# A fourth score tile turned through DRAM, its low part on VectorE, a new hand-written order and no loops, in an attention and gated-FFN kernel

## The reference, cut to what matters

```python
q = proj(Wq, bq) * scale; k = proj(Wk, bk); v = proj(Wv, bv)
q = apply_rotary(pos, q); k = apply_rotary(pos, k)
sim = jnp.einsum('bhid,bhjd->bhij', q, k)
sim = jnp.where(causal, -jnp.finfo(sim.dtype).max, sim)
attn = jax.nn.softmax(sim, axis=-1)
out = jnp.einsum('bhij,bhjd->bhid', attn, v)
out = out.transpose(0, 2, 1, 3).reshape(b, n, INNER)
x = x + ga * (out @ Wo + bo)
```

## Time and profile before

| | us |
|---|---|
| median of 3 runs | 970.95 |
| the profiled execution | 968.9 |
| its span | 967.0 |
| PE busy | 934.2 (97%) |
| DVE busy | 735.9 (76%) |
| ACT busy | 673.4 (70%) |
| POOL busy | 774.9 (80%) |

### The profile page before, as it was taken

The page is one execution under the profiler, slowest core; times in us unless marked ns, Lnnn a source line. Parts: engine busy times, 40 slices in busy tenths (PEclk is TensorE's granted clock), DMA queues, the critical chain, the costliest instruction groups (busy, mean ns, idle before and its releaser), DMA issues.

```text
span 967.0 us, 20178 instructions
## 1 busy us (share of the span) xinstructions
PE 934.2 (97%) x5667; PEld 833.6 (86%) x5667; DVE 735.9 (76%) x1582; ACT 673.4 (70%) x1354; POOL 774.9 (80%) x555
## 2 busy tenths in 40 slices
PE   6989999999999999999999999999999999878898
PEld 5878998888889989989998888889989989767787
DVE  6766877778878877787877877887878777867544
ACT  5766766677677767676767677777777676757763
POOL 2468988898898988898889888998889888795653
...
GB/s 256 163 137 137 179 166 142 159 182 154 140 136 175 167 136 158 179 167 150 145 156 174 169 150 133 183 148 139 156 170 168 158 147 171 177 95 44 1 44 46
DMA packets 108978, 141.63 MB, mean 146 GB/s; under 512 B 12948, under 2 KB 80084, under 8 KB 108884
## 3 DMA queue, kind: packets, MB, share of 16 engines
...
...
## 4 chain that ended last, share of the span: by engine, by line
PE 87%; DVE 3%; POOL 3%; issue 2%; ACT 2%; DMA 1%; SPq 0%; POOLq 0%; DVEq 0%; ACTq 0%
PE ps_r L1565 18%; PE ps_r L1564 18%; PE ps_r L1563 18%; PE ps_s L1563 7%; PE ps_s L1565 7%; PE ps_s L1564 7%; PE ps_t L1728 5%; PE ps_s L1570 1%; PE ps_s L1573 1%; PE ps_r L1570 1%; PE ps_r L1572 1%; PE ps_r L1668 1%; ACT probs L1046 1%; POOL pT_lo L782 1%; DMA wmod_a<-in_L_wmod 1%
## 5 line engine op out<-in xcount | busy, mean ns | idle before, releaser
L1046 ACT ACTIVATE probs<-ps_s,neg_max 128x128 f32<-128x128 f32 (+7 forms) x256 | 189.8, 742 | 84.5 <-DVE neg_max L1451 82.3
L764 POOL TENSOR_TENSOR swapped<-swapped,sin_sb 128x512 f32<-128x512 f32 x124 | 161.2, 1300 | 94.4 <-DMA swapped<-straight 94.1
L1451 DVE CUSTOM_DVE_ANT_0 ps_s<-ps_s,mask_wide 128x128 f32<-128x128 f32 (+7 forms) x256 | 193.6, 756 | 14.8 <-PE ps_s L1565 12.4
L782 POOL TENSOR_TENSOR pT_lo<-side_p,pT_hi 128x1024 fp32r<-128x1024 f32 (+2 forms) x93 | 195.3, 2131 | 0.7 <-ACT pT_hi L1035 0.7
L773 POOL TENSOR_TENSOR qk_lo<-swapped,qk_hi 128x512 fp32r<-128x512 f32 x124 | 159.4, 1297 | 19.7 <-ACT qk_hi L930 19.6
L767 POOL TENSOR_TENSOR swapped<-swapped,qk_cos 128x512 f32<-128x512 f32 x124 | 161.3, 1301 | 10.5
L1563 PE MATMUL ps_s<-qk_hi 128*128 128x512 f32 (+4 forms) x384 | 142.1, 370 | 2.4 <-ACT probs L1046 2.3
L1379 DVE STREAM_TRANSPOSE squares<-probs 128x1024 f32<-128x1024 f32 (+2 forms) x93 | 103.1, 1109 | 51.6 <-ACT probs L1046 48.4
L1565 PE MATMUL ps_r<-pT_hi,v_lo 128*128 128x512 f32 (+3 forms) x384 | 133.0, 346 | 0.0
L1564 PE MATMUL ps_r<-pT_lo,v_hi 128*128 128x512 f32 (+3 forms) x384 | 132.6, 345 | 0.0
L1565 PE MATMUL ps_s<-qk_hi,qk_lo 128*128 128x512 f32 (+4 forms) x384 | 131.4, 342 | 0.0
...
## 6 DMA issues: line engine op xcount, KB each, us to landing
...
```

The costliest lines, as they stand in the source:

```text
L764: pool.tensor_tensor(swapped[:, q, :], swapped[:, q, :], sin_sb[:, at_], ALU.mult).then_inc(rotated, 1)
L782: pool.tensor_tensor(turned_at(t, 0, t + 1)(pT_lo).rearrange("p k (i c) -> p k i c", c=SQUARE), from_squares(side_p[t], t)[:, t::-1, :, :] ...
L1046: nc.scalar.activation(halved(t, probs[:, P_AT[step] * P:(P_AT[step] + t + 1) * P]), score_rows(step, t), ACT.Exp, bias=neg_max[:, t:t + 1 ...
L1451: nc.vector.tensor_tensor_reduce(rows, rows, halved(t, mask_wide[:, SEQ - n_keys:SEQ]), -1.0, -MASKED, ALU.add, ALU.min, accum_out=neg_max ...
```

## The change

Tile 4 is turned aside as well, in units 0 to 30: its five transposes on TensorE, their two copies on ScalarE and two subtractions on VectorE are gone. In their place stand a transposition of squares on VectorE (`side:7-`), a write and four reads on SyncE (`side:7-`, `back:7-`), one copy of 640 keys per row on ScalarE (`side:7-`), and one subtraction of 640 on VectorE (`lower:7-`), for which the function `side_lower` was there and not used. All plans of the loop and of units 29 to 31 are written anew. ScalarE issues the loads of the weights. The loops are gone: units 1 to 31 stand one behind another, with constants as wait values.

```diff
-SIDE = (7, 6, 5)
+SIDE = (7, 6, 5, 4)
...
-TENSOR_PLAN = """scores:0 turn:6.0- make:K0+ make:Q0+ turn:7.0- scores:1 make:P0- scores:2 turn:7.1- make:K1+ make:Q1+
-        turn:0.0 scores:3 make:W00- scores:4 make:P1- turn:2.0 scores:5 make:W01- make:W10- turn:4.0 scores:6
-        make:W11- scores:7 make:V0 make:V1"""
...
+TENSOR_PLAN = """make:K0+ turn:6.0- scores:0 make:Q0+ scores:1 make:P0- scores:2 make:K1+ make:Q1+ turn:0.0 scores:3
+        make:W00- turn:2.0 scores:4 make:P1- make:W01- scores:5 make:W10- make:W11- scores:6 turn:4.0 make:V0
+        scores:7 make:V1"""
+SCALAR_PLAN = """exp:7- out:K0+ turn:6.0- out:Q0+ exp:0 side:5- high:P0- exp:1 out:K1+ exp:2 out:Q1+ side:7- high:K0+
+        turn:0.0 split:V turn:2.0 exp:3 high:Q0+ split:Q exp:4 split:K high:P1- side:1 | exp:5 raw:K split:O
+        high:K1+ exp:6 raw:Q high:V0 turn:4.0 side:3 raw:V high:Q1+ high:V1 raw:O"""
+VECTOR_PLAN = """side:7- max:0 cos:K0+ turn:6.0- cos:Q0+ max:1 | low:P0- max:2 side:1 cos:K1+ cos:Q1+ lower:7- max:3
+        sum:W00- turn:0.0 max:4 side:3 split:Q turn:2.0 low:P1- sum:W01- max:5 sum:W10- max:6 side:5 sum:W11-
+        low:V0 max:7 turn:4.0 low:V1"""
+POOL_PLAN = """side:5- rotate:K0+ rotate:Q0+ low:K0+ split:V low:Q0+ rotate:K1+ rotate:Q1+ split:K low:K1+ split:O |
...
-SYNC_PLAN = """swap:K0+ swap:Q0+ | side:1 back:1 side:3 swap:K1+ swap:Q1+ back:3 side:5 back:5 raw:K raw:Q raw:V raw:O"""
+SYNC_PLAN = """side:7- swap:K0+ swap:Q0+ back:7- | side:1 back:1 swap:K1+ side:3 swap:Q1+ back:3 side:5 back:5"""
...
+            def load_raw(ps, j, n):
+
+                if j == WO:
+                    act.wait_ge(w_ready[WV], ps.passes(n + 1))
+                    src = wo_t[:, bass.ds(ps.passes(n) * 2, 2), :]
+                else:
+                    act.wait_ge(w_ready[WO if j == WV else j], ps.passes(n))
+                    src = w_t[j][:, :, bass.ds(ps.passes(n) * 2 * DH, 2 * DH)]
+                act.dma_start(w_buffers[j][0], src).then_inc(raw_ready[j], 16)
...
             run(Span(0, 1))
-            with act.Fori(0, LAST) as i:
-                run(Span(1, 1 + UNITS, i))
-            run(Span(1 + LAST * UNITS, ALL_UNITS + 1))
+            run(Span(1, ALL_UNITS + 1))
```

More of the change, by code:

```diff
@@ L130 @@
 PLANS_29 = {
-    SYNC_PLAN: """swap:K0+ swap:Q0+ | side:1 back:1 side:3 swap:K1+ swap:Q1+ back:3 load:0 side:5 back:5 load:1"""}
+    SYNC_PLAN: """side:7- swap:K0+ swap:Q0+ back:7- | side:1 back:1 swap:K1+ side:3 swap:Q1+ back:3 load:0 side:5 back:5
+        load:1"""}
 PLANS_30 = {
-    TENSOR_PLAN: """scores:0 turn:6.0- make:K0+ make:Q0+ turn:7.0- scores:1 make:P0- scores:2 turn:7.1- make:K1+ make:Q1+
-        turn:0.0 scores:3 make:W00- scores:4 make:P1- turn:2.0 scores:5 make:W01- make:L0 make:W10- make:L1
-        turn:4.0 scores:6 make:L2 make:W11- make:L3 scores:7 make:L4 make:L5""",
@@ L138 @@
[L138 to L142, removed]
+    TENSOR_PLAN: """make:K0+ turn:6.0- scores:0 make:Q0+ scores:1 make:P0- scores:2 make:K1+ make:Q1+ turn:0.0 scores:3
+        make:W00- turn:2.0 scores:4 make:P1- make:W01- scores:5 make:W10- make:L0 make:W11- make:L1 scores:6
+        turn:4.0 make:L2 make:L3 scores:7 make:L4 make:L5""",
@@ new lines @@
+    SCALAR_PLAN: """exp:7- out:K0+ turn:6.0- out:Q0+ exp:0 side:5- high:P0- exp:1 out:K1+ exp:2 out:Q1+ side:7- high:K0+
+        turn:0.0 turn:2.0 exp:3 high:Q0+ float:0 exp:4 float:1 high:P1- side:1 float:2 exp:5 out:L0 high:K1+
+        out:L1 exp:6 turn:4.0 out:L2 side:3 out:L3 high:Q1+ out:L4 out:L5""",
+    VECTOR_PLAN: """side:7- max:0 cos:K0+ turn:6.0- cos:Q0+ max:1 low:P0- max:2 side:1 cos:K1+ cos:Q1+ lower:7- max:3
+        sum:W00- turn:0.0 max:4 side:3 turn:2.0 largest:0 low:P1- sum:W01- max:5 sum:W10- max:6 side:5 sum:W11-
@@ L151 @@
-    SCALAR_PLAN: """out:K0+ exp:7- turn:6.0- exp:0 out:Q0+ side:5- turn:7.0- turn:7.1- float:3 high:P0- turn:0.0 exp:1 exp:2
-        high:P1- exp:3 turn:1.0 turn:1.1 turn:2.0 exp:4 gated:0 out:D0 turn:3.0 exp:5 turn:3.1 turn:4.0 out:D1
[L153 to L156, removed]
@@ L157 @@
-    SYNC_PLAN: """load:4 load:5"""}
+    TENSOR_PLAN: """make:K0+ make:Q0+ scores:0 turn:6.0- scores:1 make:P0- scores:2 turn:0.0 scores:3 make:W00- make:P1-
+        turn:1.0 scores:4 turn:1.1 turn:2.0 make:W01- make:X scores:5 make:D0 turn:3.0 make:W10- turn:3.1
+        turn:4.0 make:W11- scores:6 make:D1 turn:5.0 scores:7 make:D2 turn:5.1""",
+    SCALAR_PLAN: """out:K0+ exp:7- turn:6.0- exp:0 out:Q0+ side:5- float:3 high:P0- exp:1 turn:0.0 exp:2 side:7- exp:3
+        high:P1- turn:1.0 turn:1.1 turn:2.0 exp:4 gated:0 out:D0 turn:3.0 exp:5 turn:3.1 turn:4.0 out:D1 exp:6
+        turn:5.0 out:D2 turn:5.1""",
@@ L160 @@
+    VECTOR_PLAN: """side:7- max:0 turn:6.0- max:1 low:P0- max:2 largest:2 turn:0.0 max:3 lower:7- sum:W00- largest:3 low:P1-
+        turn:1.0 turn:1.1 max:4 moments:0 turn:2.0 sum:W01- width:X max:5 turn:3.0 sum:W10- turn:3.1 turn:4.0
+        sum:W11- max:6 max:7 turn:5.0 turn:5.1""",
+    SYNC_PLAN: """side:7- back:7- load:4 load:5"""}
 ENDING = {
```

38 lines of the change are left out of this document (8 added, 30 removed).

## The result

The changed kernel takes 978.95 us (median of 6 runs, 978.31 to 985.3), the kernel before 970.65 beside it: 8.3 us slower, where 13 us faster was forecast. The ratio over all runs is 1.0104, with a 95% interval of 1.0084 to 1.0124; that of the medians alone is 1.0086. The two longest runs (985.3 and 984.82) had a mean granted clock of 0.983 and 0.985, the other four 0.994 or 0.995.

A forecast was written before the change was run, and what follows sets the result against it. TensorE's own work was taken as the bound: 968.9 us, less 16.0 for transposes, plus 2.9 for late V0, gave 955.8; with 2.05 from profiled run to median, 957.9, rounded 958. The range was 951 to 980.

The forecast's parts named there:

- What bounds the kernel: Middle units: TensorE's own work sets the 25.90 us per unit, so what leaves TensorE is gained until a wait appears.
- the transposes: TensorE, units 2 to 30: five transposes gone, 0.55 us per unit, 29 units, 16.0 us gained.
- The low part of tile 4: VectorE before P1: waits about 0.1 us for GpSimd, within 0.3 us of slack, so no stall.
- both sums: From V0's end: GpSimd ends Q0's first operation 14.1 us later, VectorE's low part comes due 14.07 later; trusted to 0.3.
- rival B: Some units stall as GpSimd's phase shifts with weight splits and DMAs; 965, or 963 to 969 us; chance 0.2.
- rival C: GpSimd begins Q0's second operation before VectorE's low part; P1 1.0 us late every unit, 987 us; chance 0.2.
- D: Rival: tile 4's read-backs come late through SyncE's order or fuller DMA queues, delaying ScalarE; 968 to 975 us; chance 0.08.
- The sums: V0 waits for VectorE's sum of W10: 0.1 us late in 29 units, +2.9 us, ends 0 and 4.4.
- The ends: Unit 1 and behind unit 30, where TensorE already has gaps: nothing gained, 2 us to either side.
- ScalarE's and SyncE's DMAs: ScalarE's four weight loads a pass: 0 taken, 3 us kept for the range; SyncE's added transfers and later swap: nothing.
- The loops: Removing the seven rounds of the loops gives TensorE nothing; VectorE's and ScalarE's register arithmetic goes, which helps the margins.

The follow-up runs named there:

- q0_small: The changed kernel with GpSimd's two operations on Q0 cut to 16 of 512 elements from unit 2 on, leaving out most of that rotation; 964.86 us.
- combo_sums: Changed kernel with previous orders in units 1, 30, 31, tile 4's low part one place earlier, SyncE's weight loads, VectorE's W10 and W11 sums earlier; 1000.56 us.
- flat_actload: The kernel before, without loops and with ScalarE issuing the weight loads; tile 4 and the order as before; 972.66 us.
- order_only: The changed kernel (its order, no loops, ScalarE's weight loads) with tile 4 turned on TensorE again; 984.82 us.

## Why the prediction was wrong

**What bounds the kernel, and the transposes: right.** A unit without a stall is 25.56 in the changed kernel and 25.58 in q0_small. With the 0.17 of V0 and V1 off that is 25.4, the forecast's 25.35 within 0.06.

**The low part of tile 4: this step failed**, where it said "I take no stall here". The duration and the exclusion held. So did both sums, for one unit: V0 ended at 352.98, GpSimd's first operation of Q0 at 367.12, 14.14 later (forecast 14.1), and VectorE began L1389 at 367.06, 14.08 later (14.07). VectorE's sum held on: 14.0 to 14.2 in all middle units but one. GpSimd's did not: 14.1 to 15.8. What failed is that the sum starts GpSimd on ScalarE's high Q1, as if GpSimd then stood waiting, and lets it run on from there without a wait. POOL 14 us earlier, in the unit without a stall and in the one with it:

```profile
355.64 1.30 POOL L767 TENSOR_TENSOR qk_lo<-swapped,qk_hi 128x512 fp32r<-128x512 f32 x1 [1.04 <-ACT qk_hi L922]
```

```profile
379.68 1.31 POOL L767 TENSOR_TENSOR qk_lo<-swapped,qk_hi 128x512 fp32r<-128x512 f32 x1
380.94 1.30 POOL L750 TENSOR_TENSOR wo_lo<-wo_raw,wo_hi 128x512 fp32r<-128x512 f32 x1
382.19 1.29 POOL L767 TENSOR_TENSOR qk_lo<-swapped,qk_hi 128x512 fp32r<-128x512 f32 x1
```

V0 ended at 352.98 and at 378.47. In the first GpSimd waits and takes low Q1 2.66 later; in the second it comes from the split of Wo and takes it 3.72 later, 1.06 late, and everything up to Q0 with it. The split is not the whole of it. Shortly before, GpSimd had waited 2.33 us for the swapped keys of K1 (to 374.30), where 1.3 to 1.6 is usual, and that left it no pause to take up the split in. The five units of the middle with both, a split of Wo and a wait of some 2.1 us or more, stall 3.6 us together; the two with such a wait and no split (L1389 at 678.94 and 782.30) don't stall.

In four other units low Q1 began on time, and GpSimd waited for a DMA afterwards, 0.44 to 1.66 us: twice for the swapped keys of K0, twice for tile 5, whose read-back ScalarE's copy awaits. ACT and POOL in the worst, whose P1 came 1.1 late at 525.06:

```profile
517.53 0.85 ACT L1027 ACTIVATE pT_hi<-side_p 128x768 fp32r<-128x768 f32 x1 [1.80 <-DMA side_p<-side_out]
```

```profile
518.45 1.84 POOL L776 TENSOR_TENSOR pT_lo<-side_p,pT_hi 128x768 fp32r<-128x768 f32 x1 [1.66 <-ACT pT_hi L1027]
```

All four come 15 to 19 us behind ScalarE's loads, and have 2.8 us of the stalls. That the loads made those DMAs late is not shown; two other units at the same distance have no such wait.

The stalls of P1, from its starts, add up to 8.8 us in 19 of 27 units, 0.33 a unit. This is rival B's pattern with the exclusion of rival C, and a part of D's late transfers. But C had GpSimd too early, with the second operation of Q0 begun; the runs show it too late, with the first not ended, in every stalled unit of the middle. C had its 1.0 in every unit, and needed 0.45. The Trainium skill (SBUF — State Buffer, § Who interferes with whom) has the exclusion that made this; the miss is in the phase, not in the rule.

**The sums: V0 right, V1 overlooked.** From the transposes of tile 2 to V0's second matmul the changed kernel takes 0.50 and combo_sums, with its earlier sums, 0.45: V0 is 0.05 late (forecast 0.1). For V1, from the last matmul of the scores, it is 0.39 and 0.27, so 0.12 late, by the sum of W11, which the prediction did not follow. Together 0.17, so 4.6 us over 27 units where 2.7 was counted.

**The ends failed by more than the stall**: "I take nothing, with 2 us to either side" were 4.0 and 5.3. Of the start, flat_actload gives 1.7 to ScalarE's early loads and q0_small 2.2 to GpSimd's operations on Q0; order_only starts even later without tile 4, so the parts don't simply add. Of the ending, 1.4 is the clock, and q0_small is 1.7 shorter than the changed kernel beyond that; 2.2 are left, of which order_only has 1.6 without tile 4 (166.3 less 2.8 of clock, against 161.9). PE in the changed kernel at the start and in the ending, gaps that the kernel before does not have there, or has at 0.57 us (its P1 at 855.08):

```profile
98.56 0.50 PE L1563 MATMUL ps_r<-hT_hi,w_hi 128*128 128x512 f32 x1 [1.89 <-DVE v_lo L1296]
...
864.33 0.50 PE L1563 MATMUL ps_s<-qk_hi 128*128 128x512 f32 x1 [1.41 <-ACT probs L1038]
...
867.97 0.47 PE L1563 MATMUL ps_r<-pT_hi,v_hi 128*128 128x512 f32 x1 [1.42 <-DVE pT_lo L1389]
```

The orders of units 30 and 31 were written anew, and the prediction read only that of the middle.

**ScalarE's and SyncE's DMAs: right on the issue, wrong on the traffic.** The issue is hidden. Where the loads go out was not weighed, and it decides up to 5.8 us, in either direction.

**The loops: right**, nothing.

The account of the spans: 953.9 forecast (967.0 less 16.0 plus 2.9), 976.9 measured, 23.0 missing. The start and the ending are 9.3 of it (1.4 by the clock), with another 0.9 for the two units of the 29 that lie in them; the stalls of P1 are 8.8; V1 and the rest of the order 0.07 x 27 = 1.9; 2.1 stay unexplained. q0_small is 6.3 us faster than the kernel before, but 5.3 of its gain over the changed kernel lie at the start and in the ending (1.4 by the clock): the stalls of the middle alone, taken away, would have brought the change no further than about even.

What stays open: which instructions in the orders of units 30 and 31 cost the 2.2 us of the ending that neither the clock nor GpSimd's operations on Q0 explain. They were not taken apart further.
